# First group's taps, step sizes and injections moved ahead in the prologue, with the staged weights laid out anew

## The chip, the cores and the metric

One Trainium2 chip, of which the kernel uses one core. The metric is the device time of one execution in microseconds (us). All arithmetic is float32.

## The reference

The input is 64 sequences of 128 tokens and 256 channels, with one 128x128 adjacency per sequence. Two layers follow one another, each on a layer norm of its input and added to it:

```python
# layer 1, attention over a graph and three hops
Xw = X @ Wv + bv;  sj = Xw @ aw[:d];  si = Xw @ aw[d:]
e = leaky_relu(sj[:, None, :] + si[:, :, None] + ab, 0.2)
alpha = A * exp(e);  transition = alpha / (sum(alpha, -1) + 1e-12)
H = 0;  Xk = X
for k in range(3):
    H = H + Xk @ Wk[k] + bk[k];  Xk = transition @ Xk
x1 = x + relu(H)
# layer 2, a selective state space (1024 channels, 16 states) between two linear maps
h = norm(x1) @ W_fc1.T + b_fc1
u, z = split(h @ W_in.T);  u = silu(conv4(u) + conv_b)
dt, B, C = split(u @ W_xproj.T);  delta = softplus(dt @ W_dt.T + b_dt)
h_t = exp(delta_t * A) * h_(t-1) + delta_t * u_t * B_t;  y_t = h_t . C_t
out = x1 + ((y + u * D) * silu(z)) @ W_out.T @ W_fc2.T + b_fc2
```

## The kernel before

The 64 sequences are worked in 32 groups of two. The matrices W_fc1 and W_in are multiplied into one at run time ("folds": `fold_in`, L717 to L723), since nothing nonlinear stands between them, and W_out and W_fc2 likewise (`fold_wo`). The fold has a half for u (n = 0 to 3) and one for z (n = 4 to 7), and a row of biases for each (`fold_bias`, L725 to L730), which is copied to a row in SBUF (`bias_row`), stored to DRAM and loaded back as a column (`bias_column`, SP).

The order of the work is written out by hand and is the same program on all engines. `walk` runs bodies k = -3 to 31, each of 32 steps v. In body k, group k is scanned (32 units, one a step), group k+1 has its dense part, and groups k+2 and k+3 have their graph part (`graph_steps`: in body k the steps v+22 of group k+2 up to v = 15, and the steps v-10 of group k+3 from v = 10). The bodies -3 to -1 have no scan; they are the prologue. What an engine does in a step stands in its queue in that order, and each engine works its queue strictly in order; between engines there are semaphores.

The dense part of a group, as `dense_pe`, `dense_act`, `conv` and the POOL's body have it, by step: four u products (-1, 2, 4, 6; each is evacuated by ACT and then has six taps on DVE, L1013), `sequence_starts` on POOL (8), the SiLU of u (10), the projection to dt, B and C (11, 12; PE L864), its copy (14), four step-size products (15 to 21; PE L875) with an Abs and a Relu each, two Exps (19, 23), one Ln (25, L596), four z products (26 to 29; L853) with an evacuation each (L566), POOL's delta (27, L411) and du (28, L419) and the first injections (29, 31; L429), the first decays on ACT (31; L505). The scan itself is DVE L988, the product with C is POOL L438, the sum over states PE L796.

The graph part of a group, by its own steps: transpose (6), the edge product e (9; L907 and L909), its Relu and Exps (11; L654 to L658), POOL's two products (12; L376, L379), row sums (14) and their reciprocal on DVE (15; L1048), a hop product (16; L947) and its copy (18), the spread of the reciprocal (19), the scaled matrix att (20; DVE L1051), hops and the new x1.

In the prologue of before, group 0 has its dense part in body -1, at the steps above, and z's folds lie at (-2, 6), (-1, 1), (-1, 3) and (-1, 5), their bias rows at (-1, 7) and (-1, 9). The graph part of group 2 begins in body -1 at v = 10, and DVE's `att` of it (v = 30) stands in the queue before the first scan (body 0, v = 0).

All weights that are only needed for folding are staged in the tile `bc`, which holds B and C later. They are loaded by two queues: SP's (q1: `GRAPH_LOADS`, then x and the adjacency) and ACT's (q10: `FOLD_LOADS`, then `DENSE_LOADS`). DVE's first copy (L966) waits for all of `GRAPH_LOADS`, and the whole program behind it. In `GRAPH_LOADS`, aw and bv have rows of 16 and 8 bytes.

## Time and profile before

| | |
|---|---|
| runs | 3718.7, 3723.0, 3727.8 us (median 3723.0) |
| profiled execution | 3724.0 us, of which the span is 3722.2 us |
| mean granted TensorE clock | 0.989 of full speed |
| busy, share of the span | DVE 94%, POOL 93%, PE 92%, ACT 80% |
| first scan begins | at 167.25 us of the span |

Times in the rows below are microseconds from the start of the span.
### The profile page before, as it was taken

To read this page: it belongs to the slowest core of one execution; us is meant where nothing else is said; L and a number is where in the kernel's file an instruction comes from. 1 tells how busy PE (TensorE), PEld (TensorE's weight loads), DVE (VectorE), ACT (ScalarE), POOL (GpSimd) and SP (SyncE) were. 2 spreads that over 40 slices of the span, in tenths; PEclk is the share of its full clock that TensorE was granted. 3 is DMA by queue.
4 is the path that set the end of the run, shared out by engine and by line. 5 is a ranking of instruction groups with operands and counts; after the bars stand their busy time and mean duration, and the time that the engine had idled before them with its cause. 6 is when DMAs were issued, how large, how long until landed. Compare 5 with 4: busy or idle time off the path is not lost.

```text
span 3722.2 us, 43792 instructions
## 1 busy us (share of the span) xinstructions
PE 3433.3 (92%) x11130; PEld 1959.2 (53%) x11130; DVE 3496.5 (94%) x2813; ACT 2975.3 (80%) x6611; POOL 3456.8 (93%) x1767
## 2 busy tenths in 40 slices
PE   5899999999999999999999999999999999999887
PEld 3555555555555555555555555555555555555443
DVE  0499999999999999999999999999999999999998
ACT  2588878888888888888888888888888888888774
POOL 0299999999999999999999999999999999999998
PEclk9899999999999999999999999999999999999999
DMA  3111101111101111100111110111110111110110
GB/s 112 53 56 59 59 9 53 56 58 58 59 9 53 56 59 58 58 29 33 56 58 58 59 44 18 58 56 58 58 59 4 58 56 58 59 54 9 46 51 9
DMA packets 50720, 183.68 MB, mean 49 GB/s; under 512 B 7356, under 2 KB 33220, under 8 KB 42086
## 3 DMA queue, kind: packets, MB, share of 16 engines
q1 hardware_dynamic: 48898, 174.17, 12.1%
q10 hardware_dynamic: 1636, 7.83, 0.5%
q14 instruction: 168, 1.38, 0.1%
q8 instruction: 18, 0.29, 0.0%
HBM read 164.15 MB, written 17.83 MB: 49 GB/s over the span
## 4 chain that ended last, share of the span: by engine, by line
POOL 46%; issue 30%; PE 18%; DVE 4%; ACT 2%; POOLq 1%; DMA 0%; SPq 0%; DVEq 0%; ACTq 0%
POOL st L438 31%; POOL st L429 9%; PE y_ps L796 8%; PE d_ps L853 3%; POOL delta L411 3%; POOL du_sb L419 2%; DVE st L988 2%; PE g L816 1%; PE g L947 1%; DVE st L976 1%; PE d_ps L864 1%; ACT dec L505 1%; POOL rstd L396 1%; POOL att L376 1%; POOLq L193 1%
## 5 line engine op out<-in xcount | busy, mean ns | idle before, releaser
L438 POOL TENSOR_TENSOR st<-st,bc 128x1024 f32<-128x1024 f32 x1024 | 2404.9, 2366 | 97.8 <-DVE st L988 97.2
L988 DVE TENSOR_TENSOR_SCAN st<-dec,st 128x1024 f32<-128x1024 f32 x1024 | 2308.8, 2272 | 11.9 <-ACT dec L505 7.1
L796 PE MATMUL y_ps<-st,ident 128*128 128x512 f32 x4096 | 1932.5, 605 | 158.2 <-POOL st L438 156.8
L505 ACT ACTIVATE dec<-delta,decay 128x254 f32<-128x254 f32 x4096 | 1696.2, 466 | 239.6 <-DVE st L988 236.6
L796 PEld LDWEIGHTS y_ps<-st,ident 128*128 128x128 f32 x4096 | 747.3, 191 | 984.4 <-issue 657.5
L976 DVE TENSOR_TENSOR st<-du,bc 128x1024 f32<-128x1024 f32 x736 | 882.4, 1199 | 12.9 <-PE y_ps L796 12.4
L429 POOL TENSOR_TENSOR st<-du_sb,bc 128x1024 f32<-128x1024 f32 x288 | 681.8, 2368 | 0.1
L833 PE MATMUL d_ps<-xnT,wxz 128*128 128x256 f32 x1024 | 249.4, 387 | 71.4 <-DVE u L1013 70.7
L1013 DVE SCALAR_TENSOR_TENSOR u<-d_ps,chan,u 128x250 f32<-128x250 f32 (+2 forms) x768 | 305.9, 465 | 7.8 <-ACT u L553 7.8
L553 ACT ACTIVATE u<-d_ps,bconv,chan 128x256 f32<-128x256 f32 x256 | 130.0, 558 | 215.7 <-PE d_ps L833 215.7
L833 PEld LDWEIGHTS d_ps<-xnT,wxz 128*128 128x128 f32 x1024 | 191.7, 191 | 156.1 <-DVE u L1013 105.0
L853 PE MATMUL d_ps<-xnT,wxz 128*128 128x256 f32 x1024 | 243.6, 381 | 3.2 <-ACT zs L566 3.2
L853 PEld LDWEIGHTS d_ps<-xnT,wxz 128*128 128x128 f32 x1024 | 194.7, 191 | 84.1 <-issue 43.3
L816 PE MATMUL g<-wo,zs 128*128 128x256 f32 x1024 | 235.2, 382 | 0.8 <-DVE zs L995 0.8
L816 PEld LDWEIGHTS g<-wo,zs 128*128 128x128 f32 x1024 | 191.8, 190 | 64.7 <-issue 39.3
L947 PE MATMUL g<-wks,xT 128*128 128x256 f32 x768 | 200.6, 391 | 1.4 <-DVE rinv L1048 0.9
L947 PEld LDWEIGHTS g<-wks,xT 128*128 128x128 f32 x768 | 146.4, 194 | 70.9 <-issue 52.8
L566 ACT ACTIVATE zs<-d_ps,bxz 128x256 f32<-128x256 f32 x256 | 106.7, 467 | 95.1 <-PE d_ps L853 94.9
L585 ACT ACTIVATE delta<-d_ps,chan 128x256 f32<-128x256 f32 x256 | 121.7, 475 | 62.5 <-PE d_ps L875 61.5
L411 POOL TENSOR_TENSOR delta<-delta,relu 128x512 f32<-128x512 f32 x128 | 163.5, 1277 | 4.6 <-ACT delta L596 4.6
L419 POOL TENSOR_TENSOR du_sb<-delta,u 128x512 f32<-128x512 f32 x128 | 164.0, 1281 | 0.1
L875 PE MATMUL d_ps<-dbc,rows 32*128 32x256 f32 x512 | 145.3, 403 | 2.5 <-ACT relu L586 2.5
(113 smaller groups left out, 2560.0 us busy)
## 6 DMA issues: line engine op xcount, KB each, us to landing
bc<-bc_dram SPq DMA_DIRECT2D x64, 2048.0 KB, 9.8
xg<-x_dram SPq DMA_DIRECT2D x32, 256.0 KB, 11.4
x_dram<-xg SPq DMA_DIRECT2D x32, 256.0 KB, 2.0
last_x<-x_dram SPq DMA_DIRECT2D x32, 256.0 KB, 2.6
out_dram<-last_x SPq DMA_DIRECT2D x32, 256.0 KB, 2.1
bc<-w_inT_dram ACTq DMA_DIRECT2D x1, 4096.0 KB, 13.9
adjt<-adjT_dram SPq DMA_DIRECT2D x32, 128.0 KB, 11.1
bc<-w_out_dram ACTq DMA_DIRECT2D x1, 2048.0 KB
```

The costliest lines, as they stand in the source:

```text
L411: nc.gpsimd.tensor_tensor(delta[:, r, 2 * i:2 * i + 2, :], delta[:, r, 2 * i:2 * i + 2, :], relu[:, 2 * i:2 * i + 2, :], ALU.add).then_inc ...
L429: nc.gpsimd.tensor_tensor(st[:, sl, :, :, :], du_sb[:, i % 2, None, :, :].to_broadcast([P, SU, 2, T]), bc[:, r, 0, SU * q:SU * q + SU, Non ...
L438: nc.gpsimd.tensor_tensor(st[:, sl, :, :, :], st[:, sl, :, :, :], bc[:, p, 1, SU * q:SU * q + SU, None, :].to_broadcast([P, SU, 2, T]), AL ...
L505: a = nc.scalar.activation(dec[:, v % 2, s, j, :].rearrange("p (b t) -> p b t", b=PAIR)[:, :, 1:], delta[:, p, 2 * i + j, :].rearrange("p ...
L796: mm = nc.tensor.matmul(y_all, ident[:, :], st[:, sl, s, :, :].rearrange("p j t -> p (j t)"), start=False, stop=(q == Q - 1 and s == SU - ...
L816: mm = nc.tensor.matmul(o_ps[:, b, :], zs[:, p, j, b * L:(b + 1) * L], wo[:, j, :], start=False, stop=(j == J - 1), skip_group_check=True)
L833: mm = nc.tensor.matmul(d_ps[:, j % 2, :], wxz[:, c, j * P:(j + 1) * P], xnT[:, r, c, :], start=(c == 0), stop=(c == KC - 1))
L853: mm = nc.tensor.matmul(d_ps[:, j % 2, :], wxz[:, c, INNER + j * P:INNER + (j + 1) * P], xnT[:, r, c, :], start=(c == 0), stop=(c == KC - 1))
L947: mm = nc.tensor.matmul(g0[:, b * DIM:(b + 1) * DIM], xT[:, c, b * L:(b + 1) * L], wks[:, n, c, :], start=(opens and c == 0), stop=(closes ...
L976: nc.vector.tensor_tensor(st[:, sl, :, :, :], du[:, None, :, :].to_broadcast([P, SU, 2, T]), bc[:, p, 0, SU * q:SU * q + SU, None, :].to_b ...
L988: nc.vector.tensor_tensor_scan(h, dec[:, v % 2, :, :, :].rearrange("p s j t -> p (s j t)"), h, 0.0, ALU.mult, ALU.add).then_inc(S["scanned ...
L1013: nc.vector.scalar_tensor_tensor(dst, src, chan[:, m, j:j + 1], dst, ALU.mult, ALU.add)\
```

## The change

Group 0 has its u products and taps in body -2, at v = 16, 19, 22, 25 (evacuation and taps one step behind each). The rest of its dense part stays in body -1 but nine steps sooner: `dense_pe`, `dense_act` and POOL's conditions are called with v + 9. The folds of z are moved from before the projection to between and behind the step-size products, at v = 7, 9, 11 and 13 of body -1, their bias rows at 14 and 15. The graph parts stay at their steps. In SP's queue the store and the two broadcast loads of B and C of group 0 (`b_and_c`) come before x1's store and the second bias column. DVE's constants for the taps move to body -2.

So that B and C can be loaded sooner, the staging is laid out anew: W_in^T is loaded in two parts, u's half (16 KB a partition, as four rows of 4 KB) and z's half (the same, as the second of `DENSE_LOADS`), where before it was one load with rows of 32 KB. W_fc1 and W_fc2 are staged in the tile `zs`.

```diff
+U_OF_0, U_READY_OF_0 = (16, 19, 22, 25), (17, 20, 23, 26)
-Z_FOLDS = {(-2, 6): 4, (-1, 1): 5, (-1, 3): 6, (-1, 5): 7}
-Z_BIAS = {(-1, 7): 2, (-1, 9): 3}
+Z_FOLDS = {(-1, 7): 4, (-1, 9): 5, (-1, 11): 6, (-1, 13): 7}
+Z_BIAS = {(-1, 14): 2, (-1, 15): 3}
+SOONER = 9
...
-        s_winT = staged(HC, 2 * INNER).rearrange("p (c e) -> p c e", c=HC)
-        s_fc1 = staged(HC, DIM).rearrange("p (c e) -> p c e", c=HC)
-        s_wout = staged(HC, INNER).rearrange("p (c e) -> p c e", c=HC)
-        s_fc2T = staged(HC, DIM).rearrange("p (c e) -> p c e", c=HC)
+        s_winU = staged(HC, INNER).rearrange("p (c e) -> p c e", c=HC)
...
+        at[0] = 2 * STATE * T
+        s_winZ = staged(HC, INNER).rearrange("p (c e) -> p c e", c=HC)
+        s_wout = staged(HC, INNER).rearrange("p (c e) -> p c e", c=HC)
+        late = zs[:, 1, :, :].rearrange("p j t -> p (j t)")
...
-        FOLD_LOADS = [(s_fc1, w_fc1), (s_winT, w_inT), (s_bfc1, b_fc1)]
+        FOLD_LOADS = [(s_fc1, w_fc1), (s_winU, w_inT[:, :, 0:INNER]), (s_bfc1[:, :], b_fc1)]
         DENSE_LOADS = [
-            (s_alog, a_log),
+            (s_alog, a_log), (s_winZ, w_inT[:, :, INNER:2 * INNER]),
...
+                if dense and not scan:
+                    b_and_c(sp, k + 1, 1 - p)
                 if ends:
...
+                if dense and not scan:
+                    bias_column(sp, 1)
                 if has_previous(k) and scan:
...
+                if isinstance(g, int) and g == 0:
+                    sp.wait_ge(S["folded"], FOLDS // 2)
+                    sp.wait_ge(S["bias_row"], 2)
+                    sp.wait_ge(S["decay_exp"], 1)
...
             def body(pe, k, p, scan, dense, ends, begins):
                 r = 1 - p
-                if dense and not scan:
-                    pe.wait_ge(S["w_dense"], 16 * len(DENSE_LOADS))
                 for v in range(U):
                     if dense:
-                        dense_pe(pe, k + 1, r, v, ends)
-                    if ends and v + 1 == U:
+                        dense_pe(pe, k + 1, r, v if scan else v + SOONER, ends, scan)
+                    if ends and not dense and v in U_OF_0:
+                        u_of_0(pe, p, U_OF_0.index(v))
+                    if ends and dense and v + 1 == U:
                         first_u(pe, k + 2, p)
...
             def body(act, k, p, scan, dense, ends, begins):
...
-                    if dense and v in U_READY:
+                    if ends and not scan and not dense and v in U_READY_OF_0:
+                        evacuate_u(act, 0, p, U_READY_OF_0.index(v))
+                    if dense and scan and v in U_READY:
                         evacuate_u(act, k + 1, r, U_READY.index(v))
                     if scan and v + 1 < U:
                         decays(act, k, p, v + 1)
-                    if dense and v + 1 == U:
+                    at = v if scan else v + SOONER
+                    if dense and at + 1 == U:
                         decays(act, k + 1, r, 0)
                     if dense:
-                        dense_act(act, k + 1, r, v)
+                        dense_act(act, k + 1, r, at)
```

TensorE's queue in body -1, before, from the last fold of z to the third step-size product (y_ps<-bc folds, d_ps<-xnT,wxz the u product, y_ps 1x512 the bias rows, d_ps<-u,wx the projection, d_ps<-dbc,rows step sizes, g<-ident,xn transposes of groups 1 and 2):

```order
L721 MATMUL y_ps<-bc 128x512 x4
L833 MATMUL d_ps<-xnT,wxz 128x256 x4
L728 MATMUL y_ps<-bc 1x512 x8
L864 MATMUL d_ps<-u,wx 64x256 x8
L892 MATMUL g<-ident,xn 128x128 x4
L875 MATMUL d_ps<-dbc,rows 128x256 x2
L892 MATMUL g<-ident,xn 128x128 x4
L875 MATMUL d_ps<-dbc,rows 128x256 x4
```

The same place in the changed program, from the first step-size product to the third z product (L903 step sizes, L740 folds, L920 transposes, L747 bias rows, L881 z products):

```order
L903 MATMUL d_ps<-dbc,rows 128x256 x2
L740 MATMUL y_ps<-bc,zs 128x512 x4
L903 MATMUL d_ps<-dbc,rows 128x256 x2
L740 MATMUL y_ps<-bc,zs 128x512 x4
L903 MATMUL d_ps<-dbc,rows 128x256 x2
L740 MATMUL y_ps<-bc,zs 128x512 x4
L903 MATMUL d_ps<-dbc,rows 128x256 x2
L920 MATMUL g<-ident,xn 128x128 x4
L740 MATMUL y_ps<-bc,zs 128x512 x4
L747 MATMUL y_ps<-bc,s_bfc 1x512 x8
L920 MATMUL g<-ident,xn 128x128 x4
L881 MATMUL d_ps<-xnT,wxz 128x256 x12
```

All four folds and both bias rows of z now stand behind the projection and before the first z product.

ACT's queue in body -1, before, from the second Exp of the step sizes to the first decays (L596 Ln, L566 z's evacuation, L647 and L641 copies for group 2's hops, L491 copy of du):

```order
L592 ACTIVATE delta<-delta 128x1024
L596 ACT_TABLE_LOAD
L596 ACTIVATE delta<-delta 128x2048
L566 ACTIVATE zs<-d_ps,bxz 128x256 x2
L647 ACTIVATE xn<-ident,rinv 128x128 x2
L566 ACTIVATE zs<-d_ps,bxz 128x256 x2
L641 ACTIVATE x2k<-g 128x512
L566 ACTIVATE zs<-d_ps,bxz 128x256 x4
L491 ACTIVATE du<-du_sb 128x512
L505 ACT_TABLE_LOAD
L505 ACTIVATE dec<-delta,decay 128x2x127 x8
```

ACT's queue now, from the Ln (L615) to the first decays (L518; L489 is the last bias row, L585 z's evacuation, L656 to L677 group 2's xT, Relu and Exps):

```order
L615 ACT_TABLE_LOAD
L615 ACTIVATE delta<-delta 128x2048
L489 ACTIVATE st<-y_ps 1x512
L585 ACTIVATE zs<-d_ps,bxz 128x256 x2
L656 ACTIVATE xT<-g 128x512
L585 ACTIVATE zs<-d_ps,bxz 128x256 x6
L673 ACTIVATE x1k<-g,c 128x256
L675 ACT_TABLE_LOAD
L675 ACTIVATE att<-g0,c0 128x256
L677 ACTIVATE x1k<-x1k 128x256
L504 ACTIVATE du<-du_sb 128x512
L518 ACTIVATE dec<-delta,decay 128x2x127 x4
```

Group 2's Exps stood before the Ln (among the step sizes) and now stand behind z's last evacuation, and its copies x2k and xn behind the first decays.

DVE's queue now, from z's folds to the first scans (L1068 copies of the folds, L1074 to L1080 group 2's row sum, reciprocal and att, L1006 injection, L1018 scan):

```order
L1086 SCALAR_TENSOR_TENSOR xg<-g,xg 128x512
L1068 COPY wxz<-y_ps 128x512 x4
L1074 TENSOR_SCALAR rowsum<-g 128x2
L1077 RECIPROCAL rinv<-rowsum 128x2
L1080 TENSOR_TENSOR att<-g,att 128x256
L1006 TENSOR_TENSOR st<-du,bc 128x1024
L1018 SCALAR_TENSOR_TENSOR st<-dec,st 128x1024 x2
```

The last five of them stand in the same order as before; what moved is what stands ahead of them.

## Rows read from the trace of the kernel before

**Rows 1.** Windows, core 0: busy time by engine, clock, DMA share.

```profile
167.25:280.00 112.75, 104.46 (x354) 63.37 (x353) 108.73 (x87) 95.02 (x213) 103.22 (x53) 0.97 0.12 46
```

**Rows 2.** DMA queues, window 4.8 to 13.5 us: packets, MB, share of 16 engines.

```profile
q10 hardware_dynamic: 114, 3.74, 101.2%
q1 hardware_dynamic: 121, 0.00, 0.8%
```

**Rows 3.** DMA queues, window 13.5 to 18.6 us.

```profile
q1 hardware_dynamic: 832, 1.22, 64.8%
```

**Rows 4.** Timeline, DVE then ACT: start, us, what, idle before.

```profile
18.54 0.43 DVE L966 COPY bc<-bc 128x512 f32<-128x512 f32 x1 [16.98 <-DMA rows<-bk_dram]
...
5.67 4.50 ACTq L450 DMA_DIRECT2D rows<-w_dtT_dram  x1
```

**Rows 5.** Timeline, PE then ACT, first group becomes ready.

```profile
79.90 0.66 PE L892 MATMUL g<-ident,xn 128*128 128x128 f32 x4 [2.26 <-ACT xn L632]
...
81.09 1.08 ACT L632 ACTIVATE xn<-xg,shift,rstd 128x256 f32<-128x256 f32 x2
```

**Rows 6.** Timeline, PE, a product at 0.5 clock, then that window.

```profile
92.06 3.78 PE L947 MATMUL g<-wks,xT 128*128 128x256 f32 x8 [0.45 <-DVE rinv L1048]
...
93.00:95.00 2.00, 2.00 (x6) 1.57 (x5) 0.00 (x0) 0.00 (x0) 0.00 (x0) 0.50 0.00 0
```

**Rows 7.** Timeline, PE, two u steps.

```profile
104.90 1.99 PE L833 MATMUL d_ps<-xnT,wxz 128*128 128x256 f32 x8
...
110.46 1.99 PE L833 MATMUL d_ps<-xnT,wxz 128*128 128x256 f32 x8
```

**Rows 8.** Timeline, ACT then PE, around the SiLU.

```profile
125.01 0.59 ACT L476 ACTIVATE relu<-y_ps 1x512 f32<-1x512 f32 x1 [2.50 <-PE y_ps L728]
...
127.40 1.28 ACT L570 ACT_TABLE_LOAD   x1
...
130.65 3.67 PE L864 MATMUL d_ps<-u,wx 128*64 128x256 f32 x16 [1.32 <-ACT u L570]
```

**Rows 9.** Timeline, PE, a fold with its neighbour, then a step-size product.

```profile
116.13 3.60 PE L721 MATMUL y_ps<-bc 128*128 128x512 f32 x8
119.56 1.89 PE L833 MATMUL d_ps<-xnT,wxz 128*128 128x256 f32 x8
...
134.84 1.12 PE L875 MATMUL d_ps<-dbc,rows 32*128 32x256 f32 x4
```

**Rows 10.** Timeline, ACT and SP, logarithm and bias rows; the tile view's landing line.

```profile
151.96 1.91 ACT L596 ACTIVATE delta<-delta 128x2048 f32<-128x2048 f32 x1
...
131.10 0.25 SPq L322 DMA_DIRECT2D bias_dram<-relu  x1
132.33 0.36 SPq L325 DMA_DIRECT2D bxz<-bias_dram  x1
...
DMA to landing us min/median/max: 2.1/2.2/2.3
```

**Rows 11.** Timeline, ACT, the evacuations of z; window of one edge product.

```profile
157.06 0.84 ACT L566 ACTIVATE zs<-d_ps,bxz 128x256 f32<-128x256 f32 x2 [1.88 <-PE d_ps L853]
...
159.98 0.84 ACT L566 ACTIVATE zs<-d_ps,bxz 128x256 f32<-128x256 f32 x2 [1.59 <-PE d_ps L853]
...
44.60:46.75 2.15, 2.14 (x17) 1.00 0.00 0
```

**Rows 12.** Timeline, ACT then DVE, group 2 up to the reciprocal and beyond.

```profile
147.37 0.41 ACT L658 ACTIVATE x1k<-x1k 128x256 f32<-128x256 f32 x1
...
97.28 0.42 DVE L1051 TENSOR_TENSOR att<-g,att 128x256 f32<-128x256 f32 x1 [5.27 <-PE g L923]
...
150.28 0.17 DVE L1048 RECIPROCAL rinv<-rowsum 128x2 f32<-128x2 f32 x1
```

**Rows 13.** Timeline, DVE, the last steps before the first scan.

```profile
164.34 1.22 DVE L976 TENSOR_TENSOR st<-du,bc 128x1024 f32<-128x1024 f32 x1 [0.56 <-ACT du L491]
167.25 4.47 DVE L988 TENSOR_TENSOR_SCAN st<-dec,st 128x1024 f32<-128x1024 f32 x2 [1.68 <-ACT dec L505]
```

## What was predicted

> **What bounds the kernel now.** I read the page first, then the windows, then the chain of waits and the timelines up to 168 us. Once the scans run, DVE and POOL are both nearly full: in the 112.75 us of group 0's scans DVE is busy for 108.73 and POOL for 103.22 [rows 1]. The change touches no instruction there, and bodies 1 to 31 are the same code; so what it can move is the time of the first scan, 167.25 us [rows 13], and all that follows moves with it one for one. Within body 0 nothing starts that does not follow a scan or DVE's queue behind it. So the prediction is the sum up to the first scan. The chain of waits is of little help there, since it credits long stretches of group 2's graph part to "issue"; the timelines of the engines show what released what.
>
> Two things are to be seen in them. First, the program starts only at 18.54, when DVE's first copy has the last of SP's weight loads; it had stood idle for 16.98 us [rows 4]. Second, in DVE's queue the first scan stands behind group 2's reciprocal and its `att`. In before this costs nothing: the reciprocal is at 150.28 [rows 12], the injection for unit 1 at 164.34, and the scan then waits 1.68 us more for ACT's decays [rows 13], which come behind the last evacuation of z.
>
> **The start (S).** SP's queue q1 and ACT's q10 are served in turn: from 4.8 to 13.5 us q10 moved 114 packets and q1 121 [rows 2], one for one, but q10's were 3.74 MB (32.8 KB each, the rows of W_in^T) and q1's next to nothing, the 8 and 16 byte rows of bv and aw. So 8.7 us went into getting 121 tiny packets through. With 4 KB rows the same 121 turns carry 0.5 MB, which at the 3.74 MB in 8.7 us of that window is 1.2 us: 7.5 us saved. Against it, q1's last two large loads (identity and wk, 128 packets each, in the 1.22 MB of [rows 3]) now have 256 packets of 4 KB beside them, about 1 MB more than before: 2.2 us at the same rate. Net -5.3. ACT may take some of it back: its issues stalled for 4.50 us behind the queue's backlog [rows 4], and it now issues 512 + 512 rows in place of 128. It has to be through, with a table load of 1.28 [rows 8], when the attention products behind DVE's copy are done. I count 0.6 for that and take S = -4.7; the bounds are -5.5 and 0 (ACT's issue so late that nothing is won).
>
> By the Trainium skill (DMA: Bandwidth & Descriptors, "Queues, rings and completion order") each DMA engine switches between queues only at packet boundaries, and one packet typically holds 9 to 17 descriptors. If the rows of one load counted as one such packet, q1 would need one turn for each load, and 4 KB rows would change little: S near 0 to -1. This case's trace speaks against it, since its records alternate row by row (121 to 114).
>
> **From the start to group 0 ready.** Unchanged but for one fold more or less on PE, which ends before it is needed. I go on in the clock of before's trace and add S at the end. The transposes end at 80.56 [rows 5], the copy of xnT before ACT's 81.09 [rows 5] ends at 81.2, and the first u product can start, in body -2, at 81.2.
>
> **Taps and projection.** A round of u product, evacuation and taps took 110.46 - 104.90 = 5.56 us at full clock [rows 7]. At 0.50 a product of eight records takes 3.78 [rows 6] in place of 1.99 [rows 7]; PE is idle ahead of these transposes, for longer than the 2.26 us of [rows 5], as the fold that stood there is gone, so I give the first round 5.6 + 1.8 = 7.4. The rounds start at 81.2, 88.6, 94.2 and 99.7. Group 1's edge product (2.1 us [rows 11]) fits in a round's gap. Behind the fourth u product (101.7) come group 1's hop product (like 1.99; 103.6), its copy (0.6; 104.2), and then group 2's moments, which stand ahead of the SiLU in ACT's queue: from 125.5, behind the bias row's 125.01 + 0.5, to the table load at 127.40 they take 1.9 [rows 8]: 106.1. The last taps (99.7 + 5.5 = 105.2) and POOL's edge are not later. Table load to projection 130.65 - 127.40 = 3.25, projection 3.67 [rows 8]: 113.1, where before it was 134.3. B and C can start then, and have over 30 us.
>
> **Step sizes and folds.** PE goes on without a gap. Group 1's last hops take 3.7 (from the u product's end, 110.46 + 1.99 [rows 7], to the fold at 116.13 [rows 9]): 116.8. Then four step-size products of 1.12 and four folds of 119.56 - 116.13 = 3.43 [rows 9], with transposes of 0.66 [rows 5]: 18.9, to 135.7. DVE copies the last fold (0.7, a little over ACT's 0.59 for as much [rows 8]), the first bias row takes a fold's time and a copy of 0.6 [rows 8]: 140.4. Only then may ACT go on in its queue: xnT (0.5), xn (1.08) [rows 5], table load 1.28 [rows 8] and Ln 1.91 [rows 10]: 145.2, where before it was 153.87. So the step sizes are 8.7 us sooner, and no more, because the Ln now stands behind z's folds.
>
> **A new wait.** The second bias row is copied behind the Ln (145.7), and z's first evacuation of group 0 waits for that column. Store to load was 132.33 - 131.10 = 1.23, load to landing 2.2 [rows 10]: with the start, 3.5, so 149.2. In before the column landed at 134.5, and the Ln ended at 153.87 [rows 10]. Behind it on ACT stand three more evacuations, group 2's xT and Exps, and the decays. The evacuations go at 159.98 - 157.06 = 2.92 each [rows 11]: 149.2, 152.1, 155.0. The fourth z product stands behind group 2's edge product (2.1 [rows 11]): 157.1 to 159.1, evacuated by 159.95. Group 2's Relu and Exps, each like the 0.41 of [rows 12], and their table load make 2.4: 162.35, where before they ended at 147.78 [rows 12]. From there to the reciprocal's end it was 150.45 - 147.78 = 2.7 [rows 12]: 165.0. Hop product at full clock 1.9: 166.9. From the end of that product (92.06 + 3.78 [rows 6]) to att's (97.28 + 0.42 [rows 12]) 1.86: 168.8. Injection 1.22 [rows 13]: the first scan at 170.0. ACT's first decays are ready by 164.5, so DVE's queue decides, not they.
>
> That is 2.8 us later than before. PE's idle stretches, from z's first product to 149.2 and from 159.1 to 164.5, are such as had the clock at 0.50 behind them in before [rows 6]; at 1.9 for each product hit, I count two: +3.8. The bounds are -1.9 (not even the first round is slow) and +9.5 (three z products, edge and hop product). Sum: 2.8 + 3.8 - 4.7 = +1.9. On the profiled execution's 3724.0 (span 3722.2) that is 3725.9; that execution was 1.0 above the median of the runs, 3723.0, so I predict 3724.9 us. No change can be told: 0.3% is 11.2 us, about what a measurement of this kernel can tell from no change.
>
> **The rivals.**
> - *The gain goes through* (0.05). The first scan follows the Ln as in before, and group 2's graph part does not stand in the way. Then it comes 8.7 sooner, with S 13.4: 3709.6. For it: that is the chain of before, where the scan waited for decays. Against it: DVE's queue, with `att` ahead of the first injection, and ACT's, with the Exps behind z.
> - *All clocks low* (0.05). From 146 on PE works in single products with gaps, and each is at 0.50: 2.8 + 9.5 = +12.3, and if ACT's issues eat the start (S = 0) the same: 3735.3, slower. It decides when more than two thirds of the five products are slow and S is above -1. Against it: in before the evacuations of z kept their pace of 2.92 [rows 11], which leaves no room for a product of 3.78, although PE idled between the products.
> - *No start won* (0.15), by ACT's issues or by the skill's rule on packets above. S = 0 to -1, the rest as forecast: +5.6 to +6.6, 3728.6 to 3729.6, still no change.
> - *Forecast* (0.75): own range 3717 to 3731, by S from -5.5 to -3 and the clock from -1.9 to +5.7 with the 3 us or so by which medians here may differ.
>
> **How the numbers follow.** The third rival and most of the forecast lie within 0.3% of before (3711.8 to 3734.1): 0.91. Faster by more: 0.05, slower by more: 0.04. The range of 3716 to 3732 holds the forecast's own range and the third rival, and leaves out the first two.
>
> **What would show it.** Right: DVE's first copy near 14 in place of 18.54; ACT's first activation near 20; the first u product near 76.5; the projection's end near 108; the Ln's end near 141; a wait of ACT for the load of bxz of some 3 us before z's first evacuation; DVE idle until group 2's `att`, and the first scan between 163 and 172. Wrong: the first copy still at 18.5 (then packets are not served row by row), DVE waiting for ACT's decays and not for `att` at the first scan, or periods of bodies 1 to 31 that differ from before.

## The result, and the profile after

The changed kernel takes 3730.6 us (median of 22 runs, 3724.4 to 3737.5), the kernel before, run beside it, 3723.9 (22 runs, 3718.6 to 3729.8). The ratio is 1.0017, with a 95% interval of 1.0012 to 1.0023: no change by the bound of 0.3%, but a small loss of some 6.7 us that so many runs can tell. Forecast were 3724.9 us, 1.9 above the median of before that was on record then (3723.0), in a range of 3716 to 3732; of the missing 4.8 us most is in one term, what the low clock costs.

The profiled execution took 3729.9 us (span 3728.1, clock 0.988). DVE's timeline begins with the copy that answers to that of before [rows 4]:

```profile
12.87 0.43 DVE L994 COPY bc<-bc 128x512 f32<-128x512 f32 x1 [11.31 <-DMA rows<-bk_dram]
...
71.69 0.69 DVE L1086 SCALAR_TENSOR_TENSOR xg<-g,xg 128x512 f32<-128x512 f32 x1 [10.18 <-PE g L968]
```

The program starts 5.67 us sooner (12.87 for 18.54), a little more than the forecast 4.7. The second row makes x1 of group 0, from which its dense part starts; before had it at 74.24. The lead there is only 2.55 us: 3.1 are lost on the way, where the code is the same (experiment 8 takes this up). The window view shows the place (busy by engine, then clock, DMA share):

```profile
57.00:67.30 10.30, 8.85 (x22) 5.94 (x20) 0.42 (x1) 2.58 (x10) 0.00 (x0) 0.50 0.00 1
```

Ten us at half clock; in before it was low there only from 61.8 to 65.2. ACT's issues of loads, which might have eaten the start, did not (timeline of ACT):

```profile
5.92 3.10 ACTq L463 DMA_DIRECT2D chan<-b_dt_dram  x1
...
15.56 1.28 ACT L466 ACT_TABLE_LOAD   x1 [15.56 <-issue]
19.40 0.38 ACT L466 ACTIVATE wj_rep<-g 128x256 f32<-128x256 f32 x1 [2.55 <-PE y_ps L709]
```

The longest stall of an issue is 3.10 us where it was 4.50 [rows 4], and ACT waits for PE, not PE for ACT. The q1 and q10 queues from 4.8 to 9.4 us, for [rows 2]:

```profile
q10 hardware_dynamic: 378, 1.55, 84.6%
q1 hardware_dynamic: 319, 0.28, 17.7%
```

Still about one for one, now at 4 KB a turn: 697 packets in 4.6 us in place of 235 in 8.7. Counts alone would allow turns of several rows on both queues. The single records of before's trace settle it: from 5.6 to 13.4 us each of q1's 94 rows has a row of 32 KB starting within 12 ns behind it, and never do more than two rows of q1 follow one another.

The dense part, ACT's timeline from the logarithm (Ln) on, for [rows 10] and [rows 11]. An evacuation is ACT's copy of a finished product out of PSUM:

```profile
143.58 1.91 ACT L615 ACTIVATE delta<-delta 128x2048 f32<-128x2048 f32 x1
145.40 0.57 ACT L489 ACTIVATE st<-y_ps 1x512 f32<-1x512 f32 x1
149.61 0.84 ACT L585 ACTIVATE zs<-d_ps,bxz 128x256 f32<-128x256 f32 x2 [3.64 <-DMA bxz<-bias_dram]
...
154.32 0.84 ACT L585 ACTIVATE zs<-d_ps,bxz 128x256 f32<-128x256 f32 x2 [3.38 <-PE d_ps L881]
159.03 0.84 ACT L585 ACTIVATE zs<-d_ps,bxz 128x256 f32<-128x256 f32 x2 [3.87 <-PE d_ps L881]
162.84 0.84 ACT L585 ACTIVATE zs<-d_ps,bxz 128x256 f32<-128x256 f32 x2 [2.98 <-PE d_ps L881]
...
165.73 0.41 ACT L677 ACTIVATE x1k<-x1k 128x256 f32<-128x256 f32 x1
```

The Ln ends 8.4 us sooner than before (145.49 for 153.87), and then nothing of it reaches the scan. First the new wait for z's bias column, 3.64 us, is there. Then z's evacuations are 4.71, 4.71 and 3.81 apart, not 2.92 [rows 11]. PE's timeline says why:

```profile
150.50 3.78 PE L881 MATMUL d_ps<-xnT,wxz 128*128 128x256 f32 x8 [3.64 <-ACT zs L585]
155.21 3.78 PE L881 MATMUL d_ps<-xnT,wxz 128*128 128x256 f32 x8 [0.93 <-ACT zs L585]
...
167.79 1.02 PE L944 MATMUL g<-ones,att 128*128 128x1 f32 x4 [4.99 <-POOL att L392]
```

z's second and third product are at half clock (3.78 us each); z's first, before the wait for the column, was still at full clock (1.89). The window over them:

```profile
149.20:159.50 10.30, 8.07 (x20) 6.09 (x21) 0.00 (x0) 2.64 (x7) 1.46 (x1) 0.50 0.12 38
```

DVE's queue from there to the first scan, for [rows 12] and [rows 13]:

```profile
169.04 0.17 DVE L1077 RECIPROCAL rinv<-rowsum 128x2 f32<-128x2 f32 x1
174.48 0.42 DVE L1080 TENSOR_TENSOR att<-g,att 128x256 f32<-128x256 f32 x1 [5.27 <-PE g L951]
174.82 1.21 DVE L1006 TENSOR_TENSOR st<-du,bc 128x1024 f32<-128x1024 f32 x1
175.95 4.46 DVE L1018 TENSOR_TENSOR_SCAN st<-dec,st 128x1024 f32<-128x1024 f32 x2
```

The scan is at 175.95 (before 167.25) and waits for nothing of ACT; what it stands behind is `att`. The 5.27 us of `att` are the hop product at half clock: at full clock the same wait is 3.48 in one of the runs below. Group 0's scans are as before [rows 1]: DVE is busy for 108.74 of 112.75 us, and group 1's first scan starts 112.37 us behind group 0's in both kernels.

```profile
175.95:288.70 112.75, 106.02 (x362) 64.56 (x361) 108.74 (x88) 92.92 (x207) 103.19 (x53) 0.98 0.12 46
```

Low clock stands ahead of the logarithm too. PE's timeline over group 0's u products, with a fold of before from the gap between two of its own [rows 7]:

```profile
79.14 3.78 PE L854 MATMUL d_ps<-xnT,wxz 128*128 128x256 f32 x8 [0.69 <-ACT xnT L688]
...
86.48 2.53 PE L854 MATMUL d_ps<-xnT,wxz 128*128 128x256 f32 x8 [2.71 <-DVE u L1042]
...
98.13 3.62 PE L854 MATMUL d_ps<-xnT,wxz 128*128 128x256 f32 x8 [2.78 <-DVE u L1042]
...
106.73 3.60 PE L721 MATMUL y_ps<-bc 128*128 128x512 f32 x8
```

The last line is before's. Its folds filled such gaps between the u products; in the changed kernel they stand behind the projection, PE waits 2.71 and 2.78 us for the taps ahead of the second and the fourth, and the first and fourth product and part of the second are at half clock.

### The profile page after: what moved, and what is told of

It reads as the page before. It is cut to its first block, busy times and chain, and to the rows that moved or that the text cites. A ratio compares the mean times of both kernels' runs of the same rounds, so it can differ in the third digit from the quotient of the medians.

```text
span 3728.1 us, 43796 instructions
## 1 busy us (share of the span) xinstructions
PE 3437.0 (92%) x11130; PEld 1960.1 (53%) x11130; DVE 3496.4 (94%) x2813; ACT 2974.6 (80%) x6611; POOL 3455.2 (93%) x1767
## 3 DMA queue, kind: packets, MB, share of 16 engines
q1 hardware_dynamic: 48898, 174.17, 12.1%
## 4 chain that ended last, share of the span: by engine, by line
POOL 48%; issue 32%; PE 13%; DVE 4%; ACT 1%; POOLq 1%; DMA 0%; SPq 0%; DVEq 0%; ACTq 0%
POOL st L451 31%; POOL st L442 9%; PE y_ps L817 6%; POOL delta L424 3%; POOL du_sb L432 3%; DVE st L1018 2%; PE d_ps L881 2%; DVE st L1006 1%; PE g L975 1%; POOL rstd L409 1%; PE g L837 1%; POOLq L199 1%; POOL att L389 1%; ACT dec L518 1%; PE d_ps L892 0%
## 5 line engine op out<-in xcount | busy, mean ns | idle before, releaser
L1018 DVE TENSOR_TENSOR_SCAN st<-dec,st 128x1024 f32<-128x1024 f32 x1024 | 2315.4, 2281 | 10.2 <-ACT dec L518 5.3
L518 ACT ACTIVATE dec<-delta,decay 128x254 f32<-128x254 f32 x4096 | 1696.1, 466 | 244.6 <-DVE st L1018 241.3
L1006 DVE TENSOR_TENSOR st<-du,bc 128x1024 f32<-128x1024 f32 x736 | 888.8, 1208 | 11.9 <-PE y_ps L817 11.9
L881 PE MATMUL d_ps<-xnT,wxz 128*128 128x256 f32 x1024 | 245.9, 384 | 5.9 <-ACT zs L585 5.9
L881 PEld LDWEIGHTS d_ps<-xnT,wxz 128*128 128x128 f32 x1024 | 196.2, 192 | 87.6 <-issue 43.3
L585 ACT ACTIVATE zs<-d_ps,bxz 128x256 f32<-128x256 f32 x256 | 106.5, 466 | 103.5 <-PE d_ps L881 99.7
L903 PE MATMUL d_ps<-dbc,rows 32*128 32x256 f32 x512 | 144.1, 400 | 0.0
```

Of the source, the lines that this page charges most:

```text
L518: a = nc.scalar.activation(dec[:, v % 2, s, j, :].rearrange("p (b t) -> p b t", b=PAIR)[:, :, 1:], delta[:, p, 2 * i + j, :].rearrange("p ...
L881: mm = nc.tensor.matmul(d_ps[:, j % 2, :], wxz[:, c, INNER + j * P:INNER + (j + 1) * P], xnT[:, r, c, :], start=(c == 0), stop=(c == KC - 1))
L1006: nc.vector.tensor_tensor(st[:, sl, :, :, :], du[:, None, :, :].to_broadcast([P, SU, 2, T]), bc[:, p, 0, SU * q:SU * q + SU, None, :].to_b ...
L1018: nc.vector.tensor_tensor_scan(h, dec[:, v % 2, :, :, :].rearrange("p s j t -> p (s j t)"), h, 0.0, ALU.mult, ALU.add).then_inc(S["scanned ...
```

## The experiments

For each kernel three numbers are read from its profile: DVE's first copy (the start), the way from it to x1 of group 0, and the way from x1 to the first scan, which holds all that the order of the dense part does. The times are medians beside before's own runs (3724.9 to 3725.9 us). "Below the changed kernel" is the plain difference of two medians taken at different times; counted from each one's own runs of before it is 1.0 us more.

**1. The start alone.** The kernel before, with the one load of W_in^T as two, whose rows are 4 KB:

```diff
-        FOLD_LOADS = [(s_fc1, w_fc1), (s_winT, w_inT), (s_bfc1, b_fc1)]
+        FOLD_LOADS = [(s_fc1, w_fc1), (s_winT[:, :, 0:INNER], w_inT[:, :, 0:INNER]),
+                      (s_winT[:, :, INNER:2 * INNER], w_inT[:, :, INNER:2 * INNER]), (s_bfc1, b_fc1)]
```

> The kernel before with one edit: W_in^T is loaded in two halves, with rows of 4 KB in place of 32 KB, and nothing else moved. Theory (the two DMA queues are served in turn, row by row, so q1's tiny rows wait behind q10's large ones): DVE's first copy comes at about 13 us in place of 18.54, and the first scan 3 to 6 us sooner than 167.25, depending on what the clock takes back on the way; the time falls by the same 3 to 6 us. Rival (the start was won by the new places of the staged weights, or a whole load counts as one turn): first copy within 1 us of 18.5 and no change.

Measured: 3719.4 us, 5.6 below before, ratio 0.9986 (0.9975 to 0.9997). DVE's timeline:

```profile
13.23 0.43 DVE L967 COPY bc<-bc 128x512 f32<-128x512 f32 x1 [11.67 <-DMA rows<-bk_dram]
...
160.14 4.47 DVE L989 TENSOR_TENSOR_SCAN st<-dec,st 128x1024 f32<-128x1024 f32 x2 [1.68 <-ACT dec L506]
```

The copy is 5.3 us sooner, and x1 to scan is 92.5 us, where before had 93.0. The 1.68 us for ACT's decays is that of [rows 13] to the digit. The first scan is 7.1 us sooner in this one profile, more than the 3 to 6 expected, since the way from the copy to x1 also took 1.3 less; the time fell by the 5.6 of the start. So the start is worth its full 5.3 to 5.7 us, and the new order lost about twice that.

**2. The same load with long rows.** The changed kernel, but with W_in^T's halves laid apart in DRAM, so that a row is 16 KB:

```diff
-        FOLD_LOADS = [(s_fc1, w_fc1), (s_winU, w_inT[:, :, 0:INNER]), (s_bfc1[:, :], b_fc1)]
+        FOLD_LOADS = [(s_fc1, w_fc1), (s_winU, w_inT[:, 0]), (s_bfc1[:, :], b_fc1)]
-            (s_alog, a_log), (s_winZ, w_inT[:, :, INNER:2 * INNER]),
+            (s_alog, a_log), (s_winZ, w_inT[:, 1]),
```

> The changed kernel with one edit: the two halves of W_in^T lie one behind the other in DRAM, so that each is loaded with rows of 16 KB in place of four of 4 KB; the bytes, their places in SBUF and the order are the same. Theory (row by row): the stretch in which q1 gets its tiny rows through takes about half of the 8.7 us that it took with 32 KB rows, so DVE's first copy comes at 15 to 17 us (12.87 in the changed kernel, 18.54 in before). Rival (the number of rows is the cost, fewer are faster): first copy at 12.9 or sooner. Time: 0 to 4 us above the changed kernel.

Measured: 3737.0 us, ratio 1.0031 (1.0021 to 1.0041), with the first copy at 17.92, later than the 15 to 17 expected; the time is 6.4 us above the changed kernel, where 0 to 4 were expected. The two queues, from 4.8 to 9.4 and from 12 to 17.5 us:

```profile
q10 hardware_dynamic: 115, 1.88, 99.6%
q1 hardware_dynamic: 90, 0.00, 1.1%
...
q10 hardware_dynamic: 162, 1.99, 84.6%
q1 hardware_dynamic: 159, 0.30, 14.0%
```

The tiny rows went through in half the time, as the bytes for each turn say: by the single records the 128 rows of bv start between 5.61 and 10.16 us, in before between 5.60 and 15.18. What I had not counted is the second: q1's last loads met the other half of W_in^T, again one for one and 16 KB a turn. That it is the row that counts, and not the amount or the order of the loads, is what this pair shows: the same bytes in the same order start 5 us apart. The Trainium skill (DMA: Bandwidth & Descriptors, "Queues, rings and completion order") has an engine drain a packet of typically 9 to 17 descriptors before it switches queues. This case's records do not show that: the turn is one row there. The two start times alone would not decide it, since a packet of several rows grows with the row as well.

**3. z's products back at their old steps.** The changed kernel, where `dense_pe` and `dense_act` test z's steps against v and not v + 9:

```diff
+                z = v if scan else v - SOONER
-                if v in Z_STEPS:
+                if z in Z_STEPS:
```

> The changed kernel with z's four products and evacuations of group 0 put back to their old steps of body -1 (26 to 29), so that group 2's edge product, its Relu and Exps, and the first decays stand ahead of them; all else as in the changed kernel. Theory (the first scan waits for group 2's att, whose Exps stand behind z's evacuations): Exps end at about 151 to 153 in place of 166.1, att at 166 to 168 (it then stands behind z's third evacuation) and the first scan at 167 to 170 in place of 175.95, so the time falls 6 to 9 us below the changed kernel and lands near before. Rival (ACT's decays or the bias column of z set the first scan): the first scan stays within 2 us of 175.95.

Measured: 3724.6 us, ratio 0.9998 (0.9987 to 1.0008), 6 us below the changed kernel. x1 to scan is 97.4 us in place of 104.3. ACT has group 2's Exps before z, and DVE's reciprocal is at 150.27, 18.8 us ahead of the changed kernel's (14.5 counted from x1). Exps, `att` and scan all come 2 to 3 us before the stretches expected, because x1 was 4.3 us sooner in this execution (experiment 8). That is the step which the prediction named: z in ACT's and PE's queues ahead of group 2. But the scan does not follow the reciprocal; the scaled matrix now stands behind z's last evacuation on PE and ACT:

```profile
150.27 0.17 DVE L1078 RECIPROCAL rinv<-rowsum 128x2 f32<-128x2 f32 x1
163.34 0.42 DVE L1081 TENSOR_TENSOR att<-g,att 128x256 f32<-128x256 f32 x1 [12.90 <-PE g L952]
164.81 4.46 DVE L1019 TENSOR_TENSOR_SCAN st<-dec,st 128x1024 f32<-128x1024 f32 x2
```

**4. z's folds back before the projection.**

```diff
-Z_FOLDS = {(-1, 7): 4, (-1, 9): 5, (-1, 11): 6, (-1, 13): 7}
-Z_BIAS = {(-1, 14): 2, (-1, 15): 3}
+Z_FOLDS = {(-2, 6): 4, (-1, 1): 5, (-1, 3): 6, (-1, 5): 7}
+Z_BIAS = {(-1, 7): 2, (-1, 9): 3}
```

> The changed kernel with z's four folds and two bias rows put back to the steps of before (one in body -2, three at 1, 3 and 5 of body -1, bias rows at 7 and 9); all else as in the changed kernel. Theory: two folds leave the chain of step sizes for stretches in which TensorE idled, so the Ln ends 1 to 3 us sooner than 145.5, and z's bias column has landed by then, so that the wait of 3.64 us before z's first evacuation is gone: first evacuation at about 144 in place of 149.6, the first scan 5 to 8 us sooner than 175.95, the time down by as much. Rival (group 2's part sets its own pace, whatever z does): the first scan moves by less than 2 us.

Measured: 3727.0 us, ratio 1.0006 (0.9995 to 1.0016), 3.5 below the changed kernel, less than the 5 to 8 expected. x1 to scan 99.2. The wait for the bias column is gone, and z's evacuations come at full clock (timeline of ACT):

```profile
144.88 0.84 ACT L585 ACTIVATE zs<-d_ps,bxz 128x256 f32<-128x256 f32 x2 [1.03 <-PE d_ps L881]
147.81 0.84 ACT L585 ACTIVATE zs<-d_ps,bxz 128x256 f32<-128x256 f32 x2 [1.60 <-PE d_ps L881]
```

The Ln was not sooner, though (75.7 us behind x1, against 73.8): with the folds out of the way the step-size products stand alone, PE waits for ACT between them, and from 134 to 144 the clock is low. What 3.64 us of wait cost is thus mixed with it: the first evacuation came only 1.2 us sooner after x1 (76.7 against 77.9), and most of the gain lies behind it, where z's second to fourth product are at full clock.

**5. The clock alone.** The changed kernel with nine products of 512 columns more on PE, whose result nothing reads, four behind z's first product and five behind its last:

```diff
+                        if v in (17, 22):
+                            pe.wait_ge(S["bias_row"], 4)
+                            for n in range(4 if v == 17 else 5):
+                                nc.tensor.matmul(y_all, ident[:, :], ..., start=True, stop=True)
```

> The changed kernel with nine more matmuls of 512 columns whose result nobody reads, in TensorE's idle stretches of body -1: four behind z's first product (while ACT waits for the bias column) and five behind z's last (while group 2's Exps and weights are made). Theory (low clock behind those idle stretches costs 5 to 6 us on the way to the first scan): z's second and third products and the hop product take 1.9 to 2.0 us each in place of 3.78, and from z's first evacuation to the first scan pass about 21 us in place of 26.3; the time falls by 4 to 6 us although work was added. Rival (the clock's price is hidden, since ACT or POOL set the pace there): that stretch changes by less than 1 us.

Measured: 3727.5 us, ratio 1.0004 (0.9995 to 1.0013): 3.1 us below the changed kernel (4 to 6 were expected), with work added. PE's timeline:

```profile
144.63 3.60 PE L789 MATMUL y_ps<-wks,ident 128*128 128x512 f32 x8
148.26 1.99 PE L885 MATMUL d_ps<-xnT,wxz 128*128 128x256 f32 x8
151.18 1.99 PE L885 MATMUL d_ps<-xnT,wxz 128*128 128x256 f32 x8 [0.93 <-ACT zs L585]
...
162.73 1.99 PE L979 MATMUL g<-wks,xT 128*128 128x256 f32 x8 [0.45 <-DVE rinv L1081]
```

And the window over z's products, at full clock:

```profile
147.40:156.70 9.30, 8.34 (x43) 6.55 (x42) 0.00 (x0) 2.97 (x7) 1.21 (x1) 1.00 0.12 40
```

x1 to scan is 99.2 us; from z's first evacuation to the scan 20.3 (147.37 to 167.64), where the changed kernel had 26.3 (149.61 to 175.95). The wait for the column is still there (3.47 us) and the work is the same but for what was added, so what is gained there is the clock's. Ahead of z's first evacuation nothing is gained: from x1 to it are 78.9 us, and the u products are slow as before (3.78, 3.65, 2.00 and 2.98). A second profile of the same kernel:

> The kernel with the nine unused products on TensorE once more, nothing edited. Two executions of the changed kernel had 104.3 and 102.6 us from x1 of group 0 to the first scan, the first execution with unused products 99.2. Theory (the products keep the clock up, and that is worth some 4 us): 98 to 100.5 again, z's evacuations at about 2.9 each, the hop product at 1.99. Rival (chance, as in the early part): 101 to 105. Median by the theory 1 to 4 us above the kernel before, by the rival 5 to 8 above.

gave x1 to scan 99.1, the hop product at 1.99 again, and a median of 3728.7, 2.8 above before (ratio 1.0007, 0.9997 to 1.0017).

**6. z's products spread over the gaps of group 2's graph part.**

```diff
+Z_OF_0 = (21, 26, 27, 30)
-                if v in Z_STEPS:
+                if z in Z_STEPS:
```

> The changed kernel with z's four products of group 0 at steps 21, 26, 27 and 30 of body -1: the first in TensorE's gap behind group 2's edge product, the last behind the spread of group 2's reciprocal, so that att no longer stands behind z's last evacuation. Theory (the first scan waits for att): from x1 of group 0 to the first scan pass 91 to 94 us, where it is 104.3 in the changed kernel and 97.4 with all of z at its old steps; the time is 8 to 12 us below the changed kernel, 2 to 6 below before. Rival (with att out of the way z's evacuations or the decays are as late): 96 us or more.

Measured: 3720.8 us, ratio 0.9990 (0.9981 to 0.9999), x1 to scan 94.0. The first scan is no longer behind z's last evacuation (166.09, the scan 165.84), but `att` still waits 10.01 us for a product of PE, and z's second product is at half clock (3.78). The median is 9.8 below the changed kernel.

**7. The same, with z's folds in PE's gaps of body -2** (one each before the taps and in two of their rounds, the last between the step-size products):

```diff
-Z_FOLDS = {(-1, 7): 4, (-1, 9): 5, (-1, 11): 6, (-1, 13): 7}
-Z_BIAS = {(-1, 14): 2, (-1, 15): 3}
+Z_FOLDS = {(-2, 6): 4, (-2, 17): 5, (-2, 23): 6, (-1, 9): 7}
+Z_BIAS = {(-1, 11): 2, (-1, 13): 3}
```

> The kernel of the run with z's products spread, with z's folds moved too: one back to body -2's step 6, two into the gaps between group 0's taps (body -2, steps 17 and 23), the last at step 9 of body -1, its bias rows at 11 and 13. Theory (TensorE's run from the projection to the bias rows, with 14 us of folds in it, sets the Ln): three folds leave it, and the Ln ends 5 to 8 us sooner after x1 of group 0 than the 73.8 us of the changed kernel; the first scan comes 84 to 89 us after that x1, the time is 4 to 8 us below the run with only z's products spread. Rival (ACT's own queue, with four pairs of Abs and Relu, moments and two table loads, sets the Ln): less than 2 us.

Measured: 3715.1 us, ratio 0.9966 (0.9955 to 0.9977), the best of all. DVE's timeline to the first scans:

```profile
150.49 0.17 DVE L1080 RECIPROCAL rinv<-rowsum 128x2 f32<-128x2 f32 x1
158.48 0.42 DVE L1083 TENSOR_TENSOR att<-g,att 128x256 f32<-128x256 f32 x1 [7.83 <-PE g L954]
159.95 2.28 DVE L1021 TENSOR_TENSOR_SCAN st<-dec,st 128x1024 f32<-128x1024 f32 x1
162.63 2.29 DVE L1021 TENSOR_TENSOR_SCAN st<-dec,st 128x1024 f32<-128x1024 f32 x1 [0.40 <-ACT dec L519]
```

The Ln ends 69.5 us behind x1, 4.3 sooner than in the changed kernel (5 to 8 were expected), z's column has landed when it is wanted, and x1 to scan is 88.4 us. The folds in the gaps also bring the u products back to full clock (PE's timeline):

```profile
83.25 4.14 PE L742 MATMUL y_ps<-bc,zs 128*128 128x512 f32 x8
87.23 1.89 PE L856 MATMUL d_ps<-xnT,wxz 128*128 128x256 f32 x8
```

The second to fourth are 1.89, 1.99 and 1.97 here, and the same in the second profile; in the ten profiles of the changed kernel and experiments 2 to 6, with no fold between them, the second took 2.5 to 3.8 us and the fourth 3.0 to 3.8. A second profile and more runs:

> The kernel with z's products spread and its folds in gaps once more, nothing edited. Its first profile had x1 58.8 us behind the first copy (clock 0.5 at 57 to 67) and the first scan 88.4 behind x1. Theory (the order is worth it, the early clock is chance): x1 to scan at 87 to 90 again, and the early part either 54 to 55 or 58.8. Rival (much of the 88.4 was a lucky clock): 91 to 96. Median by the theory 8 to 12 us below the kernel before.

gave 88.7 and 3716.8 us, 9.1 below before (ratio 0.9974, 0.9964 to 0.9983), with the Ln 68.2 us behind x1.

**8. What belongs to the order and what to the execution.** Three kernels were profiled a second time, as they stand. Each of these has a single run, so only its profile is used.

> The changed kernel once more, with nothing edited. It asks whether the two half-clock stretches of the changed kernel belong to the order of its work or to the execution. In its first profile the way from DVE's first copy to x1 of group 0 took 58.8 us (71.69 - 12.87), with the clock at 0.5 from 57 to 67, and in three kernels with the same code there it took 54.5 to 55.1. Theory A (the order of the late part decides, the early one is chance): the early way may be either near 55 or near 59, but from z's first evacuation to the first scan it takes 25 to 27 us again, with z's second and third product at 3.78. Theory B (both are chance): the late part comes out elsewhere, as near 20 as near 26. First scan by A at 172 to 176.

> The kernel with z's products at their old steps once more, nothing edited. Its first profile had x1 54.6 us behind the first copy and the first scan 97.4 behind x1. Theory A: x1 to scan at 96 to 98.5 again, whichever of 55 or 59 the early part takes. Theory B: x1 to scan anywhere from 94 to 104.

> The kernel with z's products spread once more, nothing edited. Its first profile had x1 58.8 us behind the first copy (clock 0.5 at 57 to 67) and the first scan 94.0 behind x1. Theory A: x1 to scan at 93 to 95.5 again, the early part either 55 or 59. Theory B: x1 to scan from 90 to 100.

The changed kernel again: execution 3723.7 us, x1 at 67.57 in place of 71.69, scan at 170.17 in place of 175.95. The way from first copy to x1 has two courses. In the one the clock falls at 20 to 27 us and holds at 58 to 67, and it takes 54.2 to 55.1 us; in the other it holds at 20 and falls for ten us at 57, and it takes 58.8. The windows of the second profile, beside the one shown above:

```profile
20.00:27.00 7.00, 3.04 (x7) 1.93 (x8) 0.00 (x0) 2.17 (x8) 1.10 (x3) 0.53 0.87 353
57.10:67.30 10.20, 8.31 (x33) 5.56 (x31) 0.42 (x1) 2.97 (x10) 0.00 (x0) 0.96 0.00 1
```

All three kernels that were profiled again showed both courses, and so did experiment 7's with its repeat; experiment 5's took the shorter one twice. Both courses also occur on each of the three chips of the experiments. So this belongs neither to the order of the work nor to the chip but to the execution, and it is 4.3 to 4.7 us. (Before's one profile, 55.7 with the clock low at 62 to 65, is neither.) The late part is mostly the order's, but not wholly. Theory A's figures for the changed kernel missed: from z's first evacuation to the scan it took 23.95 us, not 25 to 27, since only one z product was slow (3.48); the hop product was slow again (timeline of PE, second profile):

```profile
147.11 3.48 PE L881 MATMUL d_ps<-xnT,wxz 128*128 128x256 f32 x8 [3.46 <-ACT zs L585]
151.52 2.00 PE L881 MATMUL d_ps<-xnT,wxz 128*128 128x256 f32 x8 [0.93 <-ACT zs L585]
...
163.48 3.78 PE L975 MATMUL g<-wks,xT 128*128 128x256 f32 x8 [0.45 <-DVE rinv L1077]
```

With z at its old steps x1 to scan was 98.9 (A's 96 to 98.5 missed narrowly), with z spread 95.3 (within). So x1 to scan repeats to 0.1 to 1.7 us, while the kernels differ by up to 15. What comes behind the first scan varies as well: from it to the end of the span the fourteen profiles have 3551.7 to 3559.3 us (before 3555.0, the changed kernel 3552.1 and 3551.7, experiment 6's kernel 3558.0 and 3552.3). One execution can't show, therefore, that a later first scan ends the program as much later; that rests on the medians below.

All together (us; two values are two profiles; "sum" is first copy and x1 to scan, their means against before's 18.54 and 92.7, which is the mean of 93.0 and experiment 1's 92.5, as the code behind the loads is the same):

| kernel | first copy | to x1 | x1 to scan | sum | median against before |
|---|---|---|---|---|---|
| before | 18.54 | 55.7 | 93.0 | | |
| 1, start alone | 13.23 | 54.4 | 92.5 | -5.6 | -5.6 |
| changed | 12.87, 13.03 | 58.8, 54.5 | 104.3, 102.6 | +5.1 | +6.7 |
| 2, rows of 16 KB | 17.92 | 58.8 | 104.1 | +10.8 | +12.1 |
| 3, z at old steps | 12.85, 13.13 | 54.6, 58.8 | 97.4, 98.9 | -0.1 | -0.3 |
| 4, folds early | 13.17 | 55.0 | 99.2 | +1.1 | +2.1 |
| 5, clock kept | 13.40, 12.79 | 55.1, 54.9 | 99.2, 99.1 | +1.0 | +2.5, +2.8 |
| 6, z spread | 13.01, 12.92 | 58.8, 54.2 | 94.0, 95.3 | -3.7 | -4.2 |
| 7, and folds in gaps | 12.75, 13.61 | 58.8, 54.3 | 88.4, 88.7 | -9.6 | -9.8, -9.1 |

Two numbers of the prologue give every median to within 1.8 us. The early course is left out of the sums, and they fit without it. Left out too is that in experiments 3, 6 and 7 group 1's first scan comes 113.0 to 113.4 us behind group 0's, where it is 112.4 in the others.

## Why the prediction came out as it did

- **What bounds the kernel: right.** Nearly all of it happens before the first scan: in the changed kernel group 0's scans take what they took (112.37 us to group 1's), and the sums above meet the medians of all eight changed versions to 1.8 us.
- **The start, -4.7: right, a little small.** Measured -5.6 (12.87 and 13.03 for 18.54), beyond the lower bound of -5.5 by a hair. The 0.6 given to ACT was not needed: its table load ended 2.6 us before PE had anything for it. The mechanism, one row a turn, is shown by the single records and by experiments 1 and 2. The third rival (no start won) is refuted, though its +5.6 to +6.6 is nearest to the +6.7 measured: there the number is luck, for the start was won, and order and clock took it back.
- **The order of the dense part, +2.8 before the clock: the mechanism right.** The Ln is 8.4 us sooner as a time of the span, forecast 8.7 and with the start 13.4. Its end was to be near 141 and came at 145.5 and 142.3. Counted from x1 it is 73.8 us, forecast 71.0: of these 2.8, 2.6 are slow products of TensorE, see the next point. The wait for the bias column was forecast at 3.5 and is 3.64; the first scan stands behind group 2's `att` and waits for no decays, as forecast. Experiment 3 shows it from the other side: with z behind group 2's Exps the reciprocal is 11.3 to 14.5 us nearer to x1 and the scan 3.7 to 6.9. The first rival (the gain goes through) fails on that queue.
- **The clock, +3.8: this is the term that was mis-sized.** x1 to scan was forecast at 99.6 (93.0 + 2.8 + 3.8), and was 104.3 and 102.6, so that the first scan came at 175.95 and 170.17, the one outside and the other inside the 163 to 172 that were named. The way has two parts, which meet at z's first evacuation: the forecast has 75.0 us ahead of it and 24.6 behind it (20.8 + 3.8); measured were 77.9 and 78.7 ahead, 26.3 and 24.0 behind. So the larger part of the miss is ahead.
- **The step that failed: the tap rounds of 5.56 us.** I took them from before [rows 7], where a fold of 3.6 us kept PE at work between two u products, and counted only the first product slow, though the change takes these folds away. In the changed kernel the transposes ahead of the first product took 1.12 for 0.66, the second product 2.53 (3.48 in the second profile), the fourth 3.62 (3.15), and in the second profile the hop product behind it 2.46 for 1.89: 2.6 and 3.7 us. The bound of 9.5 left the u products out altogether. Experiment 7 has folds in these gaps again and its second to fourth u product at full clock.
- **The clock behind z's first evacuation: nearly right.** I counted two slow products; there were three in the first profile (z's second and third, the hop product, 5.5 us) and two in the second (3.4). Experiment 5 measures that part apart: with the clock held, z's first evacuation to the scan falls from 26.3 and 24.0 to 20.3, the forecast without any slow product being 20.8 (149.2 to 170.0), while the part ahead stays at 78.9. The second rival (all clocks low) expected more slow products than I did, which was right, but put them all behind z's first product, where three of its five came in one profile and two in the other; its 3735.3 wasn't reached.
- **The early clock: not in the prediction.** I carried before's clock over to x1 unchanged. One profile is one draw of courses some 4 us apart. The sums fit the medians without it; how often each kernel takes which course is not shown, so a share of the 1.6 us below may be of this kind.

What stays open: the 1.6 us between the changed kernel's sum and its median (the interval of the ratio is itself 2 us to each side), what decides between the two courses, and why the stretch behind the first scan differs by up to 7.6 us between executions.

## What to carry to other kernels

A step moved sooner gains only what every queue behind it passes on: here an Ln 8 us sooner was worth nothing, because an in-order engine still had the work of another group ahead of the first scan. The same products placed in gaps (experiment 7) ended 9.1 to 9.8 us below before; 5.6 of these are the shorter rows of one load (experiment 1), and only some 4 are the new order. Where TensorE works in single products between waits, price each one at either clock, and test with a few unused products whether the clock is the cost before moving anything. When filler work is moved away from between products, don't carry over the time that they had with it. Look for a load of tiny rows that runs beside one of very long rows on another queue: here it held up the whole program.
